# First-chunk hand-over in a one-core attention and ternary feed-forward kernel: later loads, stacks and one shift moved in the issue plan

## The chip, the core and the metric

The kernel runs on one core of one Trainium2 chip. Its time is the device time of one launch in microseconds (us), taken over several runs. One further run was profiled, and every row of a trace below is from that one execution. Engines: PE (TensorE), DVE (VectorE), ACT (ScalarE), POOL (GpSimd) and SP (the queue that issues most transfers).

## The reference

A block over 2048 tokens of 256 channels, cut to what matters:

```
xn  = layernorm(x)
q, k, v = xn@Wq, xn@Wk, xn@Wv         # 8 query heads, 2 key/value heads of 32
q, k = rope(q), rope(k)
out = softmax(causal(q k^T / sqrt(32))) @ v
geo = softmax(causal(qp[:,None] * kp[None,:])) @ v     # qp, kp: 3 channels of q, k on fixed directions
att = (out + scale_h * (geo - out)) @ Wo
z   = xn @ ternary(W_syn).T + b_syn   # 1024 wide
h   = relu(z) where z >= the 102nd largest of its row, else 0
ffn = layernorm(xn + h @ ternary(W_out).T + b_out) * gamma + beta
y   = x + att + ffn
```

## The kernel before, in words

The tokens are four chunks of 512 (`c`), each of four tiles of 128 (`t`). For each chunk the kernel normalizes x (`stat`, `eps`, `rstd`, `shift`, then `xn`), transposes it (`xT`, `xnT`), projects it (`qA`, `qB`, `qK`, `v`), rotates it (`rope`, `join`), splits q and k in a high and a low part (`khi`, `hi`, `klo`, `lo`), parks these in HBM and reads them back three times over as **stacks** (`stack_hi`, `stack_lo` into q_stack and k_stack), so that one matmul over 96 rows gives scores of full precision. A matmul `gx` gives the geometric rows, which are split (`geo_in`, `geo_hi`, `geo_lo`), scanned for running extremes (`scan`, `geo_top`) and copied by small transfers into k_geo and q_geo (`geo_rows`, `geo_dma`). A pass of 32 to 128 matmuls and DVE reductions per chunk (`S`, `red`) finds each row's maximum (`mT`, `m`). Then attention runs in 160 slots (chunk, head group, kind, key tile): `score` on PE, `exp` on ACT, a causal `cut` on POOL for diagonal tiles, and `val` and `sum` on PE. Kind 1, the geometric one, comes first in each chunk. The feed-forward part goes tile by tile beside it: `z` (PE, ACT), three `sign` passes on ACT that guess a threshold, `pick` and `hide` on DVE, `hT`, `h_hi`, `h_lo`, `fo`, then `y` on DVE and `y_out` on POOL, whose last line adds into res. The last chunk's output projection is the end.

The order of all this on every engine is a list made ahead by `build_plan`: a list scheduler that takes from each flow the key with the earliest start by written-in durations (a transfer also has a landing time in `LANDING`), and by rank where starts are close. Every engine then works its list strictly in order; what a key waits for at run time is the semaphores in the loops, not the plan's times. SP has one such list. Ahead of it stand some loads that are written out by hand: x of chunk 0, the small table, x of chunk 1, W_syn, and, in the kernel before, x of chunks 2 and 3, Wo, four broadcast rows (head scales, b_out, gamma, beta) and b_syn (together `late`). DVE's `w_sort` reorders Wq, Wk, Wv; `b_split` splits b_syn and is the first reader of the late loads; `w_next` loads W_out.

Lines of the profile that are named below: L1064 `stat`; L1080 to L1086 `w_sort`; L883 `xn`; L892 `xnT`; L968 `w_put`; L874 `t_put`; L576 `geo_rows` of the keys, which ACT issues in chunk 0 and SP later; L674 the same of the queries; L686 `geo_dma`; L653 and L656 the stacks; L1348 the projections; L1371 the `S` matmuls; L1175 and L1172 their reductions; L1234 the second half of `b_split`; L1426 the end of `fo`; L1311 `y`; L837 the end of `y_out`; L779 `cut`.

Of the kernel before, what the change touches and what calls it, by code (L numbers as in the profile page):

```python
# [12 lines left out]
P = 128  # L13
# [5 lines left out]
NCH = T // CHUNK  # L19
NT = T // P  # L20
TPC = CHUNK // P
# [24 lines left out]
           "xnT_park": 3500, "khi_park": 2200, "klo_park": 2200, "hi_park": 3500, "lo_park": 3500, "stack_hi": 8500,  # L46
           "stack_lo": 8000, "xz_in": 2300, "xb_in": 2300}
STAT_RANK = 3
# [16 lines left out]
def build_plan():  # L65
# [7 lines left out]
    def unit(flow, rank, name, ns, after=()):  # L73
        add(flow, "pe", rank, ("unit",) + name, ns, after, "full")
# [17 lines left out]
    for c in range(NCH):  # L92
# [5 lines left out]
        if c < 2:  # L98
            add("blank", "pool", 1, ("blank", c), 3600, [("rstd", c)])
        add("stat", "dve", STAT_RANK if c else 0, ("shift", c), 180, [("rstd", c)])  # L100
        for t in tiles:
            add("norm", "act", 1, ("xn", t), 400, [("shift", c)] + [("unit", "xT", c - 1, 1), ("xn_park", c - 1)] * (c > 0))
        add("park", "sp", 2, ("xn_park", c), 550, [("xn", t) for t in tiles])
# [6 lines left out]
        for s in "ABK":  # L110
            unit("proj", 2 * c, ("q" + s, c), 1790, [("xnT", c, 0), ("xnT", c, 1)] + [("w_sort",)] * (c == 0))
            add("rope", "dve", 0 if c == 0 else ROPE_RANK, ("rope", c, s), 1250, [("unit", "q" + s, c)] + [("t_put", c, i) for i in range(3)] + parked,
                empties=("q" + s, c))
        unit("proj", 2 * c, ("v", c), 1250, [("xnT", c, 0), ("xnT", c, 1)])
        add("v", "dve", 0.5, ("v_in", c), 350, [("unit", "v", c)], empties=("v", c))
# [37 lines left out]
        add("geo_k", "act" if c == 0 else "sp", 1, ("geo_rows", c, 0), 3300, [("geo_lo", c), ("geo_hi", c)])  # L153
        add("geo", "sp", 1, ("geo_rows", c, 1), 3300, [("geo_lo", c), ("geo_hi", c)] + used)
        add("geo", "sp", 1, ("geo_dma", c), 2200, [("geo_top", c)] + used)

# [20 lines left out]
    for t in range(NT):  # L177
        c = t // TPC
# [58 lines left out]

    done = {("x", 0): 5200.0, ("x", 1): 13000.0, ("x", 2): 19000.0, ("x", 3): 21000.0, ("ang_in", 0): 9500.0, ("dir_in",): 14000.0}
    done.update({("w",): 11000, ("late",): 26000, ("w_in", 0): 18000, ("w_in", 1): 19000})
    emptied_by = {}  # L240
# [97 lines left out]
def attention_and_ternary_ffn(nc, x, Wq, Wk, Wv, Wo, head_scales, W_syn, b_syn, W_out, b_out, gamma, beta,  # L338
# [25 lines left out]
    with ctx:  # L364
# [225 lines left out]
        def _(sp):  # L590
# [6 lines left out]
                         W_syn.rearrange("(a p) n -> p a n", p=P)).then_inc(up_in, 16)  # L597
            for c in range(2, NCH):
                sp.dma_start(res[:, TPC * c:TPC * c + TPC], x_rows[c]).then_inc(x_in[c], 16)
            sp.dma_start(w_o[:], Wo.rearrange("(g p) n -> p g n", p=P)).then_inc(late_in, 16)  # L600
            for t_, v_ in ((all_scales, head_scales), (b_down, b_out), (gam, gamma), (bet, beta)):
                sp.dma_start(t_[:], v_.rearrange("(o n) -> o n", o=1).broadcast_to([P, v_.shape[0]])).then_inc(late_in, 16)
            sp.dma_start(b_up, b_syn.rearrange("(o n) -> o n", o=1)).then_inc(late_in, 16)
            for key in plan["sp"]:
                k = key[0]
                if k == "m_dma":

                    c = key[1]
                    consumed(sp, ("mT", c))
                    for r, rows in enumerate((m_hi, m_lo)):  # L610
                        sp.dma_start(q_stack[STK + r:STK + r + 1, c % 2].bitcast(F32),
                                     rows.bitcast(F32)).then_inc(m_in[c], 16)
# [909 lines left out]
```

## Time and profile before

| what | value |
|---|---|
| median of 3 runs (lowest to highest) | 738.36 us (736.84 to 742.61) |
| the profiled execution's own time | 732.19 us |
| its span, first to last instruction | 730.3 us |
| around the span | 1.89 us |
| mean granted clock of TensorE | 0.974 of full speed |
| PE busy | 672.8 us |

The span is what the rows below add up to; the profiled execution was the fastest one shown, 6.2 us under the median. A busy PE is not one at its peak, since its matmuls overlap. The granted clock is a share: 0.50 is 1.2 GHz, 1.00 is 2.4 GHz.

### The profile page before, as it was taken

Reading aid. Unit: us, or ns where it says so; the run is one execution under the profiler, and the core shown is the slowest. Engines: PE = TensorE matmul, PEld = TensorE weight load, DVE = VectorE, ACT = ScalarE, POOL = GpSimd, SP = SyncE. Lnnn points to the kernel's source line nnn. Section 1 sums busy time; section 2 is a strip of 40 time slices with the busy share of each in tenths; the row PEclk is TensorE's granted clock in tenths of the full one; section 3 lists DMA queues with packets and bytes.
Section 4 is the critical chain, followed back from the end, with each engine's and each line's share of the span. In section 5 each row is a group of like instructions: output and inputs, shape, how many; then the busy total and the mean of one; then the engine's idle time right before and its main releaser. Section 6 shows DMA issues by size and latency. Waiting matters only on the chain. (4 is left out here: it accounts for less than half of the span.)

```text
span 730.3 us, 12339 instructions
## 1 busy us (share of the span) xinstructions
PE 672.8 (92%) x4424; PEld 317.3 (43%) x4424; DVE 497.2 (68%) x976; ACT 448.9 (61%) x732; POOL 238.3 (33%) x312
## 2 busy tenths in 40 slices
PE   4689898999899999998999999999899899997997
PEld 2443443434444443443434444454444455554443
DVE  7857996585768766778776776865675586766612
ACT  5435446455765444298744534789888879985553
POOL 5523445113213120232100121333443342346723
PEclk9979998999999999999999999999999899999999
DMA  8577000002700000053000000000001000000000
GB/s 241 191 190 195 11 9 1 30 2 92 189 9 2 1 1 1 3 153 63 1 5 1 1 1 1 19 29 22 23 23 31 22 22 23 16 23 9 1 1 30
DMA packets 26194, 30.81 MB, mean 42 GB/s; under 512 B 7105, under 2 KB 21313, under 8 KB 25746
## 3 DMA queue, kind: packets, MB, share of 16 engines
q1 hardware_dynamic: 24210, 29.45, 14.3%
q8 instruction: 36, 0.59, 0.3%
q10 hardware_dynamic: 1920, 0.54, 0.3%
q14 instruction: 28, 0.23, 0.1%
HBM read 17.72 MB, written 11.53 MB: 40 GB/s over the span
## 5 line engine op out<-in xcount | busy, mean ns | idle before, releaser
L935 ACT ACTIVATE probs<-scores 128x1024 f32<-128x1024 f32 (+3 forms) x320 | 270.9, 893 | 226.1 <-PE acc L1481 184.9
L1172 DVE TENSOR_REDUCE piece_max<-side 128x1 f32<-128x512 f32 x190 | 126.1, 685 | 61.3 <-PE side L1371 59.1
L1474 PE MATMUL acc<-probs,v_nat 128*32 128x512 f32 (+3 forms) x1280 | 151.9, 547 | 6.8 <-POOL probs L779 5.6
L1481 PE MATMUL acc<-probs,ones_all 128*32 128x512 f32 (+3 forms) x1280 | 152.0, 547 | 0.0
L1371 PE MATMUL side<-k_stack,q_stack 128*128 128x512 f32 (+3 forms) x316 | 120.9, 432 | 10.7 <-DVE piece_max L1172 3.2
L779 POOL TENSOR_SCALAR_AFFINE_SELECT probs<-probs 128x256 f32<-128x256 f32 x128 | 54.6, 436 | 226.3 <-ACT probs L935 225.0
L1371 PEld LDWEIGHTS side<-k_stack,q_stack 128*128 128x128 f32 x316 | 54.3, 188 | 101.3 <-DVE piece_max L1172 40.2
L1456 PE MATMUL scores<-q_stack,k_stack 128*128 128x512 f32 (+3 forms) x320 | 90.9, 387 | 5.3 <-ACT probs L935 4.9
L1175 DVE CUSTOM_DVE_ANT_0 side<-side,tail_mask 128x256 f32<-128x256 f32 (+3 forms) x126 | 61.8, 498 | 19.9 <-PE side L1371 19.2
L1474 PEld LDWEIGHTS acc<-probs,v_nat 128*32 128x32 f32 x1280 | 35.8, 111 | 78.8 <-issue 59.8
L1456 PEld LDWEIGHTS scores<-q_stack,k_stack 128*128 128x128 f32 x320 | 52.9, 190 | 36.9 <-ACT probs L935 29.8
L1460 PE MATMUL scores<-q_geo,k_geo 32*128 32x512 f32 (+3 forms) x320 | 54.2, 466 | 4.2 <-ACT probs L935 2.5
L1198 DVE RECIPROCAL d_raw<-d_raw 128x512 f32<-128x512 f32 x15 | 50.2, 3346 | 1.5 <-ACT d_raw L942 1.5
L1481 PEld LDWEIGHTS acc<-probs,ones_all 128*32 128x32 f32 x1280 | 29.5, 110 | 46.8 <-issue 44.3
L831 POOL TENSOR_TENSOR y_rstd<-y_mv,minus_half 128x1 f32<-128x1 f32 x16 | 10.4, 648 | 103.8 <-DVE y_mv L1315 103.6
L1460 PEld LDWEIGHTS scores<-q_geo,k_geo 32*128 32x128 f32 x320 | 22.3, 183 | 40.7 <-ACT probs L935 23.6
L1297 DVE SCALAR_TENSOR_TENSOR work<-z_buf,thresh 128x1024 f32<-128x1024 f32 x16 | 21.6, 1351 | 18.1 <-DVEq L1294 18.1
L1425 PE MATMUL side<-down_T,h_split 128*128 128x256 f32 x128 | 31.5, 285 | 1.9 <-DVE h_split L1304 1.9
L1304 DVE TENSOR_TENSOR h_split<-side,h_split 128x512 fp32r<-128x512 f32 x32 | 20.9, 678 | 15.9 <-ACT h_split L1029 15.9
L1426 PE MATMUL side<-down_T,h_split 128*128 128x256 f32 x128 | 30.9, 280 | 0.0
L1408 PE MATMUL side<-up_T,xs_hi 128*128 128x512 f32 x64 | 28.6, 447 | 1.2 <-DVE xs_lo L1241 0.5
L1425 PEld LDWEIGHTS side<-down_T,h_split 128*128 128x128 f32 x128 | 24.1, 188 | 7.5 <-issue 3.3
(170 smaller groups left out, 899.5 us busy)
## 6 DMA issues: line engine op xcount, KB each, us to landing
q_stack<-q_parked SPq DMA_DIRECT2D x12, 512.0 KB, 7.1
q_parked<-turned SPq DMA_DIRECT2D x8, 512.0 KB, 3.3
res<-in_L_attn_x_dram SPq DMA_DIRECT2D x4, 512.0 KB, 6.4
x_parked<-xn SPq DMA_DIRECT2D x4, 512.0 KB, 2.9
xT_parked<-xnT SPq DMA_DIRECT2D x4, 512.0 KB, 2.8
xz<-xT_parked SPq DMA_DIRECT2D x16, 128.0 KB, 2.5
xb<-x_parked SPq DMA_DIRECT2D x16, 128.0 KB, 2.2
out_dram<-res SPq DMA_DIRECT2D x16, 128.0 KB, 1.7
```

Of the source, the lines that this page charges most:

```text
L779: nc.gpsimd.affine_select(out=tri, in_=tri, compare_op=ALU.is_ge, fill=0.0, base=0, pattern=[[0, 2], [1, P]], channel_multiplier=-1).then_ ...
L935: nc.scalar.activation(probs[:, slot % 2, pair, :, off:], scores[:, pair, :, off:], ACT.Exp, scale=ATT_SCALE if kind == 0 else 1.0).then_i ...
L1172: free(nc.vector.tensor_reduce(piece_max[:, h, p:p + 1], pt, AX.X, ALU.max), ("S",) + a)
L1175: free(nc.vector.tensor_tensor_reduce(pt[:, 0:ncol], pt[:, 0:ncol], tail_mask[:, CHUNK - ncol:], 1.0, -3.0e38, ALU.add, ALU.max, piece_max ...
L1198: nc.vector.reciprocal(d_raw[:], d_raw[:]).then_inc(recip_ready, 1)
L1371: last = nc.tensor.matmul(pt[:, 0:ncol], q_stack[:, b, h, col:col + P], k_stack[:, h // HG, CHUNK * p:CHUNK * p + ncol], start=True, stop= ...
L1425: nc.tensor.matmul(pt[:, 0:C], h_hi[:, i], down_T[:, i], start=(i == 0), stop=False)
L1426: last = nc.tensor.matmul(pt[:, 0:C], h_lo[:, i], down_T[:, i], start=False, stop=(i == NN - 1))
L1456: last = nc.tensor.matmul(dst[:, off:], k_stack[:, g, P * j:P * j + P], q_stack[:, b, HG * g + h, off:], start=True, stop=True)
L1460: last = nc.tensor.matmul(dst[:, off:], k_geo[rows, P * j:P * j + P], q_geo[rows, g, off:], start=True, stop=True)
L1474: nc.tensor.matmul(acc[D * h:D * h + D, 0, off:], v_nat[:, j, g], probs[:, slot_no[a] % 2, h // 2, h % 2, off:], start=(j == 0), stop=(j = ...
L1481: last = nc.tensor.matmul(acc[D * h:D * h + D, 1, off:], ones[:, 0:D], probs[:, slot_no[a] % 2, h // 2, h % 2, off:], start=(j == 0), stop ...
```

## The change

The table and the rules of `build_plan` change, and with them the list of every engine. The loads of x for chunks 2 and 3 and the six late loads leave the hand-written start of SP's list and become keys that stand in SP's stack flow behind the first chunk's `stack_lo`, `geo_rows` and `geo_dma`. These two geometric steps of chunk 0 stand in the stack flow too. The second chunk's `shift` waits for the first chunk's rotation of k, its `xn` for `hi` of chunk 0, and its projections have rank 0.5 in place of 2. The times at which the plan takes x of chunk 1 and W_syn as landed are set earlier.

```diff
-           "stack_lo": 8000, "xz_in": 2300, "xb_in": 2300}
+           "stack_lo": 8000, "x": 5000, "late": 4000, "xz_in": 2300, "xb_in": 2300}
...
-        add("stat", "dve", STAT_RANK if c else 0, ("shift", c), 180, [("rstd", c)])
+        add("stat", "dve", STAT_RANK if c else 0, ("shift", c), 180, [("rstd", c)] + [("rope", 0, "K")] * (c == 1))
         for t in tiles:
-            add("norm", "act", 1, ("xn", t), 400, [("shift", c)] + [("unit", "xT", c - 1, 1), ("xn_park", c - 1)] * (c > 0))
+            add("norm", "act", 1, ("xn", t), 400, [("shift", c)] + [("hi", 0)] * (c == 1) + [("unit", "xT", c - 1, 1), ("xn_park", c - 1)] * (c > 0))
...
-            unit("proj", 2 * c, ("q" + s, c), 1790, [("xnT", c, 0), ("xnT", c, 1)] + [("w_sort",)] * (c == 0))
+            unit("proj", 0.5 if c == 1 else 2 * c, ("q" + s, c), 1790, [("xnT", c, 0), ("xnT", c, 1)] + [("w_sort",)] * (c == 0))
...
-        unit("proj", 2 * c, ("v", c), 1250, [("xnT", c, 0), ("xnT", c, 1)])
+        unit("proj", 0.5 if c == 1 else 2 * c, ("v", c), 1250, [("xnT", c, 0), ("xnT", c, 1)])
...
-        add("geo", "sp", 1, ("geo_rows", c, 1), 3300, [("geo_lo", c), ("geo_hi", c)] + used)
-        add("geo", "sp", 1, ("geo_dma", c), 2200, [("geo_top", c)] + used)
+        add("geo" if c else "stack", "sp", 1, ("geo_rows", c, 1), 3300, [("geo_lo", c), ("geo_hi", c)] + used)
+        add("geo" if c else "stack", "sp", 1, ("geo_dma", c), 2200, [("geo_top", c)] + used)
+        if c == 0:
+            for n in (2, 3):
+                add("stack", "sp", 1, ("x", n), 500)
+            add("stack", "sp", 1, ("late",), 4000)
...
-    done = {("x", 0): 5200.0, ("x", 1): 13000.0, ("x", 2): 19000.0, ("x", 3): 21000.0, ("ang_in", 0): 9500.0, ("dir_in",): 14000.0}
-    done.update({("w",): 11000, ("late",): 26000, ("w_in", 0): 18000, ("w_in", 1): 19000})
+    done = {("x", 0): 5200.0, ("x", 1): 10000.0, ("ang_in", 0): 9500.0, ("dir_in",): 14000.0}
+    done.update({("w",): 11000, ("w_in", 0): 16000})
...
-            for c in range(2, NCH):
-                sp.dma_start(res[:, TPC * c:TPC * c + TPC], x_rows[c]).then_inc(x_in[c], 16)
-            sp.dma_start(w_o[:], Wo.rearrange("(g p) n -> p g n", p=P)).then_inc(late_in, 16)
-            for t_, v_ in ((all_scales, head_scales), (b_down, b_out), (gam, gamma), (bet, beta)):
-                sp.dma_start(t_[:], v_.rearrange("(o n) -> o n", o=1).broadcast_to([P, v_.shape[0]])).then_inc(late_in, 16)
-            sp.dma_start(b_up, b_syn.rearrange("(o n) -> o n", o=1)).then_inc(late_in, 16)
             for key in plan["sp"]:
                 k = key[0]
+                if k == "x":
+                    c = key[1]
+                    sp.dma_start(res[:, TPC * c:TPC * c + TPC], x_rows[c]).then_inc(x_in[c], 16)
+                if k == "late":
+                    sp.dma_start(w_o[:], Wo.rearrange("(g p) n -> p g n", p=P)).then_inc(late_in, 16)
...
```

On SP, from the first chunk's parking to its geometric rows. Before (turned holds the split q and k, geo_rows and maxima the geometric rows):

```order
L632 DMA k_parked<-turned 64x512
L636 DMA q_parked<-turned 128x2x512
L632 DMA k_parked<-turned 64x512
L636 DMA q_parked<-turned 128x2x512
L674 DMA q_geo<-geo_rows 4x512 x6
L653 DMA k_stack<-k_parked 32x2x512 x2
L656 DMA q_stack<-q_parked 32x4096 x2
L653 DMA k_stack<-k_parked 32x2x512
L656 DMA q_stack<-q_parked 32x4096
L686 DMA q_geo<-maxima 4x512 x4
```

After, on SP at the same place:

```order
L642 DMA q_parked<-turned 128x2x512
L659 DMA k_stack<-k_parked 32x2x512 x2
L662 DMA q_stack<-q_parked 32x4096 x2
L629 DMA x_parked<-xn 128x4x256
L659 DMA k_stack<-k_parked 32x2x512
L662 DMA q_stack<-q_parked 32x4096
L680 DMA q_geo<-geo_rows 4x512 x6
L692 DMA q_geo<-maxima 4x512 x4
L606 DMA res<-in_L0_attn_x_dram 128x4x256 x2
L608 DMA w_o<-in_L0_attn_Wo_dram 128x2x256
```

The stacks went ahead of the six copies of L674, and x of chunks 2 and 3 and the late loads stand behind the geometric copies.

On ACT, from the first chunk's xnT (L892) to the first exponentials (L935). Before:

```order
L883 ACTIVATE xn<-res,shift,rstd 128x256 x4
L892 COPY xnT<-side 128x2x256 x2
L896 CAST turned<-turned 64x512
L901 CAST turned<-turned 128x1024
L910 COPY geo_rows<-side 8x512
L911 COPY geo_rows<-side 8x512
L922 CAST geo_rows<-geo_rows 8x1024
L968 CAST up_T<-side 128x512 x3
L576 DMA k_geo<-geo_rows 4x512 x6
L968 CAST up_T<-side 128x512
L874 COPY trig<-side 128x512 x3
```

After, on ACT at the same place:

```order
L902 CAST turned<-turned 64x512
L907 CAST turned<-turned 128x1024
L889 ACTIVATE xn<-res,shift,rstd 128x256
L916 COPY geo_rows<-side 8x512
L917 COPY geo_rows<-side 8x512
L928 CAST geo_rows<-geo_rows 8x1024
L889 ACTIVATE xn<-res,shift,rstd 128x256 x3
L974 CAST up_T<-side 128x512 x2
L580 DMA k_geo<-geo_rows 4x512 x6
L974 CAST up_T<-side 128x512 x2
L880 COPY trig<-side 128x512 x2
L898 COPY xnT<-side 128x2x256
```

The second chunk's four xn went behind `khi` and `hi`, and its two xnT behind the six issues of L576 (the second of them stands two rows further down); two w_put in place of one follow these issues.

On PE, the last 14 rows of scores, values and sums and the last tile of the feed-forward part. Before, the last `fo` (L1425, L1426) ends ahead of these rows:

```order
L1426 MATMUL side<-down_T,h_split 128x256
L1456 MATMUL scores<-q_stack,k_stack 128x512 x4
L1481 MATMUL acc<-probs,ones_all 32x512 x4
L1474 MATMUL acc<-probs,v_nat 32x512 x4
L1481 MATMUL acc<-probs,ones_all 32x512 x4
L1456 MATMUL scores<-q_stack,k_stack 128x512 x4
```

After, it ends ahead of these:

```order
L1432 MATMUL side<-down_T,h_split 128x256
L1462 MATMUL scores<-q_stack,k_stack 128x512 x4
L1487 MATMUL acc<-probs,ones_all 32x512 x4
L1480 MATMUL acc<-probs,v_nat 32x512 x4
L1487 MATMUL acc<-probs,ones_all 32x512 x4
L1462 MATMUL scores<-q_stack,k_stack 128x384 x4
L1462 MATMUL scores<-q_stack,k_stack 128x256 x4
L1480 MATMUL acc<-probs,v_nat 32x512 x4
```

Before, ten attention slots are left behind the last `fo`; after, six.

## Rows read from the trace of the kernel before

**Rows 1.** The page: span, PE's line of part 1, granted clock in 40 slices.
```profile
span 730.3 us, 12339 instructions
...
PE 672.8 (92%) x4424; PEld 317.3 (43%) x4424; DVE 497.2 (68%) x976; ACT 448.9 (61%) x732; POOL 238.3 (33%) x312
...
PEclk9979998999999999999999999999999899999999
```

**Rows 2.** Timeline from 0 us, all engines: start, us, engine, line, tiles [idle before].
```profile
6.88 0.38 SPq L595 DMA_DIRECT2D res<-in_L_attn_x_dram  x1
...
10.37 3.92 DVE L1080 COPY w_qkv<-probs 128x256 f32<-128x256 f32 x2
...
13.08 0.34 SPq L603 DMA_DIRECT2D z_buf<-in_L_ffn_b_syn_dram  x1
...
14.76 0.42 DVE L1064 BATCH_NORM_STATS2 stats<-res 128x6 f32<-128x256 f32 x1
...
15.43 0.43 DVE L1064 BATCH_NORM_STATS2 stats<-res 128x6 f32<-128x256 f32 x1
...
15.64 7.28 PE L1348 MATMUL side<-xnT,w_qkv 128*128 128x512 f32 x12 [0.77 <-ACT xnT L892]
...
20.57 2.07 ACT L883 ACTIVATE xn<-res,shift,rstd 128x256 f32<-128x256 f32 x4 [2.85 <-DMA x_parked<-xn]
...
25.86 1.07 ACT L892 COPY xnT<-side 128x512 f32<-128x512 f32 x2 [3.22 <-PE side L1340]
...
31.29 0.36 SPq L636 DMA_DIRECT2D q_parked<-turned  x1
...
32.54 3.78 SPq L674 DMA_DIRECT2D q_geo<-geo_rows  x6
32.54 4.92 ACTq L576 DMA_DIRECT2D k_geo<-geo_rows  x6
...
36.36 1.59 SPq L653 DMA_DIRECT2D k_stack<-k_parked  x2
...
39.78 1.21 DVE L1234 TENSOR_TENSOR b_up_r<-z_buf,b_up_r 1x1024 fp32r<-1x1024 f32 x1
...
40.76 2.25 SPq L686 DMA_DIRECT2D q_geo<-maxima  x4
```

**Rows 3.** Landing of L595, the load of x for chunk 1.
```profile
DMA to landing us min/median/max: 3.8/3.8/3.8
```

**Rows 4.** Timeline of PE from 36 us.
```profile
39.94 7.04 PE L1348 MATMUL side<-xnT,w_qkv 128*128 128x512 f32 x12
...
49.75 0.57 PE L1460 MATMUL scores<-q_geo,k_geo 32*128 32x512 f32 x4 [1.04 <-DMA q_geo<-maxima]
...
53.67 0.33 PE L1371 MATMUL side<-k_stack,q_stack 128*128 128x128 f32 x1
```

**Rows 5.** Window: us, busy PE, PEld, DVE, ACT, POOL (count), granted clock, DMA share, GB/s.
```profile
50.00:53.50 3.50, 3.50 (x8) 0.59 (x4) 0.00 (x0) 3.15 (x4) 0.87 (x3) 0.51 0.55 205
```

**Rows 6.** Timeline of PE from 312 us: `gx` of chunk 3 to its first `S`.
```profile
314.04 1.02 PE L1361 MATMUL side<-turned,dirs_k 128*40 128x512 f32 x2
...
334.90 0.70 PE L1371 MATMUL side<-k_stack,q_stack 128*128 128x512 f32 x2 [2.36 <-DMA q_stack<-q_parked]
```

**Rows 7.** Timeline of SP from 305 us.
```profile
325.07 0.57 SPq L656 DMA_DIRECT2D q_stack<-q_parked  x1
325.70 3.33 SPq L576 DMA_DIRECT2D k_geo<-geo_rows  x6
```

**Rows 8.** Window of the late stage, columns as in Rows 5.
```profile
500.00:700.00 200.00, 187.63 (x1361) 96.22 (x1357) 130.16 (x246) 160.22 (x293) 86.03 (x103) 0.97 0.06 19
```

**Rows 9.** Timeline of the last 40 us: y of the last tile, its end on POOL, the first cut behind it.
```profile
698.22 0.48 DVE L1311 SCALAR_TENSOR_TENSOR y<-side,w_scale,xb 128x256 f32<-128x256 f32 x1 [2.97 <-PE side L1426]
...
703.26 0.73 POOL L837 TENSOR_TENSOR res<-res,y 128x256 f32<-128x256 f32 x1
...
713.60 0.41 POOL L779 TENSOR_SCALAR_AFFINE_SELECT probs<-probs 128x256 f32<-128x256 f32 x1 [9.61 <-ACT probs L935]
```

More of the change, by code:

```diff
@@ L597, in _ @@
                          W_syn.rearrange("(a p) n -> p a n", p=P)).then_inc(up_in, 16)
-            for c in range(2, NCH):
-                sp.dma_start(res[:, TPC * c:TPC * c + TPC], x_rows[c]).then_inc(x_in[c], 16)
-            sp.dma_start(w_o[:], Wo.rearrange("(g p) n -> p g n", p=P)).then_inc(late_in, 16)
-            for t_, v_ in ((all_scales, head_scales), (b_down, b_out), (gam, gamma), (bet, beta)):
-                sp.dma_start(t_[:], v_.rearrange("(o n) -> o n", o=1).broadcast_to([P, v_.shape[0]])).then_inc(late_in, 16)
-            sp.dma_start(b_up, b_syn.rearrange("(o n) -> o n", o=1)).then_inc(late_in, 16)
             for key in plan["sp"]:
                 k = key[0]
+                if k == "x":
[3 more added lines that the diff above has]
+                    sp.dma_start(w_o[:], Wo.rearrange("(g p) n -> p g n", p=P)).then_inc(late_in, 16)
+                    for t_, v_ in ((all_scales, head_scales), (b_down, b_out), (gam, gamma), (bet, beta)):
+                        sp.dma_start(t_[:], v_.rearrange("(o n) -> o n", o=1).broadcast_to([P, v_.shape[0]])).then_inc(late_in, 16)
+                    sp.dma_start(b_up, b_syn.rearrange("(o n) -> o n", o=1)).then_inc(late_in, 16)
                 if k == "m_dma":
```

## The prediction

> **What bounds the kernel now.** I read the page first. PE is busy 672.8 of 730.3 us, and its matmuls fill every slice but the first few and the last, so the end is set by PE's list: time is gained where PE stands still or runs at half clock, nowhere else [rows 1]. Then the timeline of the first 60 us, engine by engine, since the diff acts there. What one should see is a ladder. DVE sorts the weights from 10.37 to 14.76 and the projections start at 15.64 [rows 2]. The second chunk's projections start at 39.94 and end at 48.7; PE then waits 1.04 us for the geometric rows, which SP had issued by 43.01 and which landed 6.7 us later [rows 2, 4]. Behind that gap the granted clock is 0.51 for 3.5 us, so that `gx` of chunk 1 runs at 1.2 GHz [rows 5]. The first `S` matmul comes at 53.67 [rows 4]. The third view is the border to chunk 3, where PE waits 2.36 us for stacks [rows 6], the fourth the late stage and the tail [rows 8, 9].
>
> **The loads that are moved.** From 7.26 to 13.42 SP issues nine loads in 6.2 us, W_syn's among them; eight of them, about 5.5 us, leave this place [rows 2]. Nobody waits for SP there: the first parking needs xn, and ACT's one wait on a transfer, 2.85 us for the parking of xn ahead of the second chunk's xn [rows 2], is no longer reached, since these xn now stand behind `hi` of chunk 0. Removing them is worth 0 by itself. In their new place they are issued from about 43.2 to 48.7 (the 5.5 us again), where SP had only the next angles and W_out to do.
>
> **The sort is later.** By the new list DVE takes two `stat` of chunk 1 ahead of `w_sort`. x of chunk 1 lands at 6.88 + 3.8 = 10.7 [rows 2, 3], two stats take 2 x 0.67 = 1.3 us (the step from 14.76 to 15.43), and the sort takes 4.4 us (10.37 to 14.76), so it ends at 16.4 in place of 14.76. PE, which started at 15.64, waits until 16.5: **+0.85 us**, on the path. It goes through rotations, joins and `gx` to `geo_lo`, which moves from 32.5 to 33.3. The second `shift`, which went behind the rotations, frees the first rotation from a wait for POOL, but with PE's projection late by the sort it has nothing to read sooner, so I count 0.
>
> **The stacks are earlier.** In the kernel before they are issued from 36.36, behind the six copies of L674 that take 3.78 us. Now they can go when the last parking is issued, 31.29 + 0.36 + 0.8 = 32.5, which is 3.9 us earlier [rows 2]. `geo_dma` stays behind all of it and ends near 43.2 as before (the issues are the same, only their order differs). So the stacks are there some 4 us sooner and the geometric rows at 48 to 50. This gains only what PE waited for: at most the 1.04 us of [rows 4], and only if PE is ready at 48.7.
>
> **ACT decides that it is not.** In the kernel before ACT has made both xnT of chunk 1 by 27, before the first chunk's splits. Now they come behind the six issues of L576, two `w_put` and three `t_put`. L576 cannot start before `geo_lo` at 33.3; I take 33.9, because one xn (2.07 / 4 = 0.52) went ahead of `geo_in`, and three xn and two `w_put` (1.55 + 1.07) fill the time behind `geo_hi`. The six issues hold ACT 4.92 us: 38.8. Seven copies of 1.07 / 2 = 0.535 follow, 3.75 us: 42.6 [rows 2]. The projections of chunk 1 start at 42.6 and not at 39.94: **+2.7 us**, with the +0.85 inside it. Bounds: if ACT issues at the rate at which SP did the same six at L576, 3.33 us [rows 7], and starts at 33.3, it is 40.4, or +0.5; were xn or a transpose late as well, a copy or two more, +3.7. I take the upper price of the issue, since it is the row of the same engine at the same place. The wait of 1.04 us then falls away, as the rows have landed by the time PE is done (8.8 us of projections, 51.4). The first score is 1.7 us later.
>
> The Trainium skill says, on the page "DMA: Bandwidth & Descriptors", section "Issuing engines are not separate DMA queues", that several issuing engines save only the sequencer's time for starting a transfer, usually small beside the transfer. The row speaks against "small" for copies of 8 KB: 4.92 us for six; were it nothing, the sum below would be 2.3 - 4.9 = -2.6 us.
>
> **The clock.** If PE comes from `v` straight to score and `S`, the half clock behind the gap should not occur: it cost half of 3.5 us, so **-1.7 us** [rows 5]. Nothing excludes that it falls there anyway: 0 to -1.7. I take -1.7, as the only thing before the fall is the gap.
>
> **The pass for the maxima.** Work done, not position, must be compared: at about 54 the new list has three `S` matmuls more behind it, and the balance of the terms so far, +2.7 - 1.0 - 1.7, is 0. Reductions start earlier, but `b_split` (its second half alone takes 1.21 us [rows 2]) stands now among them, on DVE, where before it ran at 39, ahead of the second chunk's rotations. PE has val and sum work mixed more evenly with `S`. I take 0, from -2 to +2.
>
> **The border to chunk 3.** The list puts `xT` and the projections of chunk 3 a slot later, and SP issues the six key rows (3.33 us) ahead of `stack_lo`, which it had issued by 325.64, ahead of them [rows 7]. PE's work from `gx` to the first `S` is nearly unchanged (one score and one sum more, two transposes less), so the 2.36 us wait stays [rows 6], and up to 2.7 us come on top (3.33 less one small read that leaves that place). The transfers of the first part are still under way then, which hides some of it: **+1.0 us**, from 0 to +2.7.
>
> **The tail.** The last `fo` stands six slots from the end and not ten. From there y and y_out take 703.99 - 698.2 = 5.8 us, and the cuts of the last four key tiles stand behind them on POOL. Before, POOL was idle for 9.61 us ahead of the first cut, at 713.60 [rows 9]. Now PE has a score, sum, val, sum and two short scores, about 5.4 us, before the value matmul that needs two cuts (2 x 0.41) behind 5.8 us. That is 6.7 against 5.4: **+1.3 us**, from 0 to +2.5.
>
> **The sum.** 2.7 - 1.0 - 1.7 + 0 + 1.0 + 1.3 = +2.3 us. On the profiled execution, 732.19 (span 730.3 and 1.89 around it), that is 734.5. The median of the runs is 6.2 us above that execution; against 738.36 it is **740.7 us**. A measurement of this kernel can tell about 1%, 7.4 us, from no change, so this is a forecast of no change.
>
> **Rivals.** First, **faster**, near 730. The issues on ACT cost 3.3 us (-1.6 or more), the even mix of `S` saves 2 us, no term at the border or in the tail (-2.3), and one or two of the other stretches of half clock, 1.7 us each, do not occur. For it: the page shows a clock under 0.9 in slices 3, 7 and 32 [rows 1], and none of these is tied to work that must stay. Against it: the head has only 1.04 us of waiting that the change names, and its gain is eaten by ACT.
>
> Second, **slower**, near 750: the feed-forward part is crowded. The new list runs the `z` of tile 3 after slot 102 where it was slot 64, and the later tiles 4 to 10 slots later, but ends only 4 later. In the late stage ACT is busy 160.2 and PE 187.6 of 200 us; PE stands 12.4 us [rows 8]. One more tile there is 8 us or so of ACT's signs, copies and relu by my estimate from what is left of ACT (40 us). It decides when the chain sign, pick, hide, hT, fo of a tile is longer than the attention work that the list put between; then PE's 12.4 us double, +12. Against it: the mean leaves room, and the list interleaves by durations near the real ones.
>
> Third, **the loads come late**, 744. `b_split` waits for b_syn, the last of the loads, issued at about 48.7. By L595, 3.8 us [rows 3], it lands at 52.5, before DVE gets there at about 53.5, and costs nothing; by the 6.7 us of the geometric rows in a full queue, and x, Wo and W_out are 2.6 MB around it, at 55.4 or later. All reductions behind it in DVE's list wait, then PE for its two banks: 2 to 4 us, over the forecast. The Trainium skill, same page, section "Rules for kernel authors", advises to issue a transfer early and wait late; it speaks against this part of the change. By that rule the result would be this rival's.
>
> Fourth, the change doesn't do what it says: the stacks' landing gates nothing, because the projections fill PE until 51. That is inside the forecast.
>
> **How the numbers follow.** Forecast 0.47, within 735 to 746; faster 0.20; slower 0.18; loads late 0.15. Low end: 740.7 less 1.6, 2, 2.3 and three stretches of clock (5) gives 729.8, and the 1% bound is 731.0; high end: 740.7 + 1.7 + 2 + 1.7 + 1.2 + half of the crowding, 6, gives 753. From 730 to 752 leaves out some 2 in 10. Faster by over 1% (under 731.0) 0.15, within 1% 0.63, slower (over 745.7) 0.22.
>
> **What would show it.** Right: the projections' first pass near 16.5 and, for chunk 1, between 42 and 43, behind ACT's L580; stacks issued at 32.5; no wait for q_geo ahead of the first score; clock 1.00 near 52; a wait on POOL's cut in the last 15 us. Wrong: chunk 1's projections at 40.5 or sooner; a DVE idle row ahead of `b_split`, released by a transfer; PE busy under 92% between 500 and 700 us.

## The result, and the profile after

The changed kernel takes 728.86 us (median of 4 runs, 725.67 to 730.76) where the kernel before takes 737.6 us (4 runs, 735.14 to 742.61): a ratio of 0.9873, interval 0.9831 to 0.9915. I had forecast 740.7 us and a range whose lower end was 730. The profiled executions lie much closer together, 730.06 against 732.19 us, so first the rows, then what separates medians and profiles.

The page of the changed kernel, answering to [rows 1]:

```profile
span 728.3 us, 12341 instructions
...
PE 676.6 (93%) x4424; PEld 318.3 (44%) x4424; DVE 495.3 (68%) x976; ACT 448.2 (62%) x732; POOL 230.8 (32%) x312
...
PEclk9788887999999999999999999999999999999999
```

PE is busy 3.8 us longer in a span that is 2.0 us shorter: it stands 51.7 us in place of 57.5, and more of its time is at half clock. The first slices are no better than before, so the gain must be elsewhere.

The timeline of the first 55 us, answering to [rows 2] and [rows 4]; ACTq and SPq are the issues of transfers:

```profile
9.70 3.51 POOL L768 MEMSET q_stack<- 32x4096 f32 x1
...
11.60 2.06 DVE L1086 COPY w_qkv<-probs 128x256 f32<-128x256 f32 x2
...
15.36 5.40 PE L1354 MATMUL side<-xnT,w_qkv 128*128 128x512 f32 x6 [0.77 <-ACT xnT L898]
...
32.25 1.34 SPq L659 DMA_DIRECT2D k_stack<-k_parked  x2
33.10 1.25 ACTq L580 DMA_DIRECT2D k_geo<-geo_rows  x1
...
34.38 2.96 ACTq L580 DMA_DIRECT2D k_geo<-geo_rows  x5
...
43.03 5.39 PE L1354 MATMUL side<-xnT,w_qkv 128*128 128x512 f32 x12 [0.77 <-ACT xnT L898]
...
50.08 0.51 PE L1466 MATMUL scores<-q_geo,k_geo 32*128 32x512 f32 x4
...
53.20 0.69 DVE L1239 CAST b_up_r<-z_buf 1x1024 fp32r<-1x1024 f32 x1 [1.18 <-DMA z_buf<-in_L_ffn_b_syn_dram]
```

The first projection starts at 15.36, 0.28 us earlier than before, and waits for xnT, not for the sort. The stacks are issued at 32.25, as computed. The second chunk's projections start at 43.03 behind ACT's six issues (42.6 was forecast), the first score has no wait, and DVE stands 1.18 us for b_syn.

Windows of the changed kernel: the first score, the border to chunk 3, the late stage (answering to [rows 5] and [rows 8]):

```profile
50.00:53.50 3.50, 3.17 (x14) 1.15 (x13) 1.84 (x9) 2.88 (x4) 2.09 (x3) 1.00 0.86 215
...
300.00:345.00 45.00, 43.61 (x284) 19.36 (x282) 30.57 (x48) 29.52 (x48) 10.81 (x11) 1.00 0.38 97
...
500.00:700.00 200.00, 191.97 (x1382) 98.25 (x1378) 137.00 (x258) 174.34 (x329) 89.48 (x107) 0.98 0.07 22
...
660.00:700.00 40.00, 39.24 (x297) 19.28 (x297) 31.17 (x58) 31.13 (x48) 24.72 (x26) 1.00 0.04 11
```

The same windows of the kernel before:

```profile
300.00:345.00 45.00, 41.29 (x263) 19.72 (x253) 34.60 (x54) 32.90 (x57) 12.64 (x9) 1.00 0.37 88
660.00:700.00 40.00, 35.48 (x268) 18.32 (x272) 25.01 (x43) 19.94 (x26) 22.50 (x23) 0.96 0.01 4
```

PE stands 2.3 us less at the border, 3.8 us less between 660 and 700, and 2.0 us less between 600 and 660. That is 8.1 us where the whole span gives 5.8: between 500 and 600 it stands 1.4 us more (92.90 us busy, before 94.29), and elsewhere the windows hold different work. ACT is busier in the last of these windows, 31.1 of 40 us against 19.9: feed-forward work that the old order had already finished now stands beside the short diagonal slots. In the old order PE waits there for POOL, for ACT, and once for the feed-forward part's own split on DVE:

```profile
661.39 1.51 PE L1474 MATMUL acc<-probs,v_nat 128*32 128x384 f32 x8 [1.77 <-POOL probs L779]
...
670.95 0.73 PE L1456 MATMUL scores<-q_stack,k_stack 128*128 128x512 f32 x2 [1.20 <-ACT probs L935]
...
681.60 0.36 PE L1425 MATMUL side<-down_T,h_split 128*128 128x256 f32 x1 [1.21 <-DVE h_split L1304]
```

Whom PE waits for from 500 us to the end (us in total, times, longest), first before, then after:

```profile
PE acc L1474 <- POOL probs L779: 4.3, 4, 2.1
PE scores L1456 <- ACT probs L935: 2.0, 3, 1.2
PE scores L1460 <- ACT probs L935: 1.2, 1, 1.2
PE side L1425 <- DVE h_split L1304: 1.9, 2, 1.2
PE side L1385 <- DVE onehot L1265: 0.9, 2, 0.7
```

```profile
PE acc L1480 <- POOL probs L785: 2.6, 4, 1.6
PE scores L1466 <- ACT probs L941: 2.0, 5, 0.6
PE scores L1462 <- ACT probs L941: 1.0, 3, 0.4
PE side L1422 <- DVE work L1303: 1.4, 3, 0.6
PE side L1414 <- DVE xs_lo L1247: 1.1, 2, 0.7
```

The waits for `probs`, those that other work beside them could fill, fall from 7.5 to 5.6 us. Over the whole span they do not fall: the same view without a window adds up to 13.0 us before and 13.5 after. What the end gained in this way, other places lost. What fell over the whole span are the waits for `h_split` (3.9 to 0.9 us), for the angles that POOL copies into `turned` (5.2 to 0.8, 3.0 of it in the first 40 us), for the stacks (2.4 to 0.2) and for q_geo (1.0 to 0).

At the border, the timeline of PE after, answering to [rows 6], with SP's list behind it, answering to [rows 7]:

```profile
323.36 1.05 PE L1366 MATMUL side<-turned,dirs_q 128*40 128x512 f32 x2
...
332.12 3.34 SPq L580 DMA_DIRECT2D k_geo<-geo_rows  x6
...
336.20 0.58 SPq L662 DMA_DIRECT2D q_stack<-q_parked  x1
...
342.90 0.70 PE L1377 MATMUL side<-k_stack,q_stack 128*128 128x512 f32 x2 [0.21 <-DMA q_stack<-q_parked]
```

The key rows do go ahead of `stack_lo`, but PE's wait is 0.21 us and not 2.36. From the last stack's issue to the end of the wait it is 6.7 us (342.90 less 336.20), where it was 9.8 (334.90 less 325.07). PE's work between `gx` and this matmul did not grow: it is busy 18.2 us there (324.25 to 342.90) and was busy 18.0 (314.04 to 334.90).

In the tail, the last y_out, the cuts behind it, and PE, answering to [rows 9]:

```profile
712.08 0.73 POOL L843 TENSOR_TENSOR res<-res,y 128x256 f32<-128x256 f32 x1
712.76 1.49 POOL L785 TENSOR_SCALAR_AFFINE_SELECT probs<-probs 128x256 f32<-128x256 f32 x4
...
713.58 1.06 PE L1480 MATMUL acc<-probs,v_nat 128*32 128x512 f32 x8 [0.28 <-POOL probs L785]
```

**Medians and profiles.** Each run's record has the mean granted clock. Over 86 runs of before, slow ones left out, its mean is 0.962, over the ten of the changed kernel 0.967. These 86 runs show what the clock is worth: a line through them falls by 4.6 us for each 0.01 of it. So the clock is 2.3 us of the 9, and at equal clock the changed kernel is 7.1 us under that line. PE standing less is 4 to 6 us of it (55.5 to 57.5 us against 51.3 to 51.7, two profiles of each). The first profile of before, at 0.974, was a lucky one: by the same line that is 5.5 of the 6.2 us to the median.

### The profile page after: what moved, and what is told of

Its sections match the earlier page's. It is cut to its first block, busy times and chain, and to the rows that moved or that the text cites. A ratio compares the mean times of both kernels' runs of the same rounds, so it can differ in the third digit from the quotient of the medians.

```text
span 728.3 us, 12341 instructions
## 1 busy us (share of the span) xinstructions
PE 676.6 (93%) x4424; PEld 318.3 (44%) x4424; DVE 495.3 (68%) x976; ACT 448.2 (62%) x732; POOL 230.8 (32%) x312
## 4 chain that ended last, share of the span: by engine, by line
PE 71%; DVE 9%; ACT 6%; POOL 5%; issue 4%; DMA 3%; SPq 1%; ACTq 1%; DVEq 0%; POOLq 0%
PE acc L1487 15%; PE acc L1480 15%; PE side L1377 11%; PE scores L1462 7%; PE scores L1466 4%; DVE piece_max L1178 4%; ACT probs L941 3%; PE side L1354 3%; PE side L1441 2%; PE side L1431 2%; PE side L1414 2%; PE side L1422 2%; PE side L1432 2%; PE side L1415 1%; DVE side L1181 1%
## 5 line engine op out<-in xcount | busy, mean ns | idle before, releaser
L1466 PEld LDWEIGHTS scores<-q_geo,k_geo 32*128 32x128 f32 x320 | 22.0, 184 | 42.6 <-ACT probs L941 29.1
L807 POOL TENSOR_TENSOR mixed<-o_raw,d_raw 128x512 f32<-128x512 f32 x8 | 10.2, 1279 | 61.3 <-DVE d_raw L1204 61.2
```

The costliest lines, as they stand in the source:

```text
L1466: last = nc.tensor.matmul(dst[:, off:], k_geo[rows, P * j:P * j + P], q_geo[rows, g, off:], start=True, stop=True)
```

## The experiments

All ratios are to the kernel before, with 95% intervals; kernels were run on the same chip as their runs of before. The profile's time of one execution is named only where it matters. The planner was given a switch for each part of the change: loads, stacks, shift, xn, proj, and times (the landing times of x of chunk 1 and W_syn set earlier). A *splice* takes the first keys of one order and the rest of another. FIRST and REST name the parts switched on in the two orders, ALL stands for all six, and UNTIL is the key at which they change over (the edits are shown in short form):

```diff
+    head = order[:order.index(UNTIL)]        # of the first order
+    fixed = head + [key for key in then if key not in head]   # then: the second order
+    plan = plan_by(FIRST, fixed)             # keys in this order on every engine
```

**The two kernels again**, unchanged.

> The changed kernel once more, on the same chip and beside the same runs of before as the two halves. All theories: 0.983 to 0.992. Its profile shows how much of the clock's half-speed stretches (47.8 us in the first profile) and of PE's idle time (51.7 us) repeats from one execution to the next: idle within 1 us, half-speed stretches anywhere from 35 to 60 us.

> The kernel before once more. Ratio 0.997 to 1.003. Theory A: PE's busy time is 5 us above the first profile's 672.8 us, by more half-speed stretches, since that execution was 5 us faster than the median; the idle time is within 1 us of 57.5 us. Rival B: it has more idle time, in the first 100 us, than the first profile showed.

0.9866 (0.9818 to 0.9914) and 1.0003 (0.9966 to 1.0039). The profile of before had PE busy 677.9 us (5.1 more than the first), standing 55.5; that of the changed kernel 678.8 and 51.3. The gain repeats. The standing repeats within 2.0 us for before, where 1 us had been expected, and within 0.4 us for the changed kernel. The extra busy time of before goes with a lower clock, 0.965 against 0.974, as theory A had it.

**Which half?** Head new up to slot 61 and late order old, then the reverse.

```diff
+FIRST, REST, UNTIL = ALL, (), ("score", 2, 1, 1, 2, 0)      # head_new
+FIRST, REST, UNTIL = (), ALL, ("score", 2, 1, 1, 2, 0)      # late_new
```

> The plan of the change up to slot 61 (c 2, head group 1, geometric, key tile 2, at about 300 us), and from there the order of the kernel before. Theory A, formed from the two traces: the gain lies behind this slot, since PE's idle time fell by 2.3 us between 300 and 345 us and by 5.7 us between 600 and 700, and only by 0.9 us in the first 60; then this kernel takes what the kernel before takes, ratio 0.997 to 1.004. Rival B: the gain lies in the first chunk's hand-over, and the profiled execution of before happened to be a good one there; then the ratio is that of the whole change, 0.985 to 0.991. Rival C: the new head costs what I predicted for it (sort +0.85, ACT +1.85, wait -1.0, clock -1.7): 1.000.

> The other half: the order of the kernel before up to slot 61, loads by hand at the start of SP's list included, and from there the order of the change. Theory A (the gain is in the new order of the late part): ratio 0.985 to 0.992. Rival B (it is in the head): 0.997 to 1.004. If both halves give some 4 us each, 0.994 and 0.994, the gain is a sum of two.

0.9981 (0.9948 to 1.0015) and 0.9990 (0.9961 to 1.0019): neither half had the gain. In head_new PE does not wait for a stack at the border at all, so the 2.36 us of that wait do not make the gain by themselves. The windows show that the second splice made a hole of its own at the border, though its late window is dense:

```profile
300.00:345.00 45.00, 39.41 (x241) 16.75 (x241) 28.55 (x46) 20.78 (x31) 7.97 (x9) 0.92 0.23 60
660.00:700.00 40.00, 39.43 (x300) 21.37 (x289) 29.86 (x57) 35.41 (x66) 24.60 (x28) 1.00 0.05 14
```

**The splice put where the two orders nearly coincide** (slot 27).

```diff
+FIRST, REST, UNTIL = (), ALL, ("sum", 1, 1, 1, 2)
```

> The order of before for the first two chunks (up to slot 27, some 180 us, the early loads included), the order of the change from there. The first attempt at this half changed over at slot 61, in the middle of the third chunk's hand-over, and its trace shows a hole of its own there: PE 39.4 of 45 us busy between 300 and 345 (43.6 in the changed kernel), gx of chunk 3 waiting 2.16 us behind a feed-forward unit, and two half-speed stretches behind it; yet 98.3 of 100 us busy between 600 and 700 (99.1 in the changed kernel, 93.3 before). Theory A, the gain is in the order behind the first two chunks: 0.986 to 0.993. Rival B, it needs the new head: 0.996 to 1.003. Rival D, the two need each other: also near 1.00, but then its window from 600 to 700 is below 96 us busy.

0.9870 (0.9827 to 0.9913): the whole gain, with the old head, its late sort, its late stacks and its early loads. Its windows are those of the changed kernel:

```profile
300.00:345.00 45.00, 43.09 (x285) 18.91 (x283) 29.75 (x47) 30.58 (x48) 10.44 (x10) 1.00 0.38 97
...
660.00:700.00 40.00, 39.08 (x295) 19.21 (x297) 31.15 (x58) 31.34 (x48) 24.72 (x27) 1.00 0.04 11
```

**Parts of the change, without a splice.** Two parts alone, and all but one.

```diff
+FIRST = ("loads", "stacks")                              # stacks_loads
+FIRST = ("times", "loads", "stacks", "shift", "proj")    # no_xn
```

> Two of the five parts: the loads and x as keys behind the stacks, and the geometric rows behind the stacks; shift, xn, the projections' rank and the two times stay as before. The planner gives with these two parts the late order of the changed kernel (from the third chunk on the same). Theory A: the whole gain, 0.983 to 0.991, whatever the head does. Rival B (the head's xn and projections carry it): 0.996 to 1.003.

> All parts of the change but one: the second chunk's xn does not wait for hi of chunk 0. The planner then falls back into the order of before from the second chunk's attention on, with the stacks ahead, the late loads, the shift and the rank of the change in its head. Theory A: no gain, 0.996 to 1.004. Rival B: 0.985 to 0.991.

stacks_loads: 0.9878 (0.9851 to 0.9906), as expected of the new late order. But no_xn is slower than before by 1.4% (1.0137, 1.0103 to 1.0171), which neither theory had. Its late order is the old one, and its first two chunks cost the 10 us: `gx` of chunk 2 starts at 197.2, where the two profiles of before have 180.9 and 184.0, and the distance stays the same from there. With `shift` behind the rotation and nothing to hold xn, ACT runs the four xn, both xnT and the split of the geometric rows ahead of `hi`, which moves from about 27 to 32.99; q_parked, the stacks and the next angles follow, and PE waits. Some 4 us are lost by 55 us; the rest comes behind it, where PE waits among others 5.0 us for POOL's probs.

```profile
38.76 1.12 PE L1429 MATMUL side<-ident,h_split 128*128 128x128 f32 x4 [4.62 <-ACT up_T L999]
41.71 1.94 PE L1364 MATMUL side<-ident,turned 128*128 128x128 f32 x8 [1.83 <-POOL turned L611]
```

So the xn part, which I had charged with the delay of the second chunk, is what keeps the other parts from costing 10 us, as far as this one kernel shows.

**The feed-forward tiles alone.** Before, with a table of slots behind which each tile may start; then only the last four tiles.

```diff
+    at = (17, 62, 63, 100, 99, 103, 102, 113, 118, 114, 114, 117, 123, 124, 126, 129)   # z_late
+        turn.append(slots[at[t] - 1])
+    for t, at in ((12, 130), (13, 136), (14, 137), (15, 140)):                          # tail_late
+        turn[t] = slots[at - 1]
```

> The kernel before, all loads and the first chunk's order as they were, with one table added: the slot behind which each feed-forward tile may start, chosen so that z and fo of every tile stand in the slots where the changed kernel has them (first fo at slot 65 for 63, the rest the same, the last at 154). From chunk 3 on its PE order is that of the changed kernel. Theory A in its sharper form: the gain is that feed-forward work is left as filler for PE in the half-empty diagonal slots near 660 us and behind them: between 600 and 700 us PE is busy 98 to 99 us, ratio 0.988 to 0.995. Rival B: 0.997 to 1.004.

> The kernel before with four numbers added: tiles 12 to 15 of the feed-forward part may start only behind slots 130, 136, 137 and 140. The PE order is that of before up to slot 124; the z of these tiles then stands at slots 132, 137, 140 and 142 (before 128, 131, 134, 137) and the last fo at slot 153 (before 150, changed kernel 154). If filler work behind 655 us is what the change gained: PE is busy 37 to 39.5 us of 40 between 660 and 700 (before 34.6 to 35.5), and the ratio is 0.991 to 0.996. If the gain lies at the border and in the middle, the ratio is 0.997 to 1.003, though the window may fill.

0.9964 (0.9940 to 0.9987) and 0.9971 (0.9944 to 0.9998): each about a quarter of the gain, below what theory A asked for, and the second only just clear of no change. From the maxima pass of chunk 3 on PE's list in z_late is that of the changed kernel, so most of the gain is not in that order alone. In tail_late the window from 660 to 700 fills to 38.54 of 40 us as expected, but the one from 600 to 660 falls to 56.88 (before 57.86 and 58.71), where the tiles held back are missing.

```profile
600.00:660.00 60.00, 56.88 (x399) 30.02 (x399) 36.99 (x69) 46.88 (x81) 22.61 (x29) 0.97 0.08 23
660.00:700.00 40.00, 38.54 (x282) 20.39 (x280) 29.93 (x53) 34.04 (x62) 21.45 (x22) 1.00 0.03 8
```

**More splices in chunk 3**, meant to tell the border from the stretch behind 600 us: the new order only from slot 96, only up to slot 96, and only up to slot 128.

```diff
+FIRST, REST, UNTIL = (), ALL, ("score", 3, 0, 1, 0, 0)      # late_new3
+FIRST, REST, UNTIL = ALL, (), ("score", 3, 0, 1, 0, 0)      # mid_new
+FIRST, REST, UNTIL = ALL, (), ("score", 3, 0, 0, 0, 0)      # tail_old
```

> The order of before for three chunks (up to slot 96, the first geometric slot of chunk 3), then the order of the change. It keeps the old border to chunk 3 with its wait of 2.36 us and two feed-forward tiles done early, and has the new places of tiles 4 to 15. Theory A as it stands: PE is busy 98 to 99 us between 600 and 700, which is 5 us less standing, and the ratio is 0.989 to 0.994. If the kernel with its z slots pinned (0.9964, also dense there) tells what this stretch alone is worth, it is 0.995 to 0.998 and the rest of the gain lies in the middle, from the third chunk's pass to the border.

> The order of the change up to slot 96, the new border to chunk 3 included, then the order of before, whose feed-forward tiles end at slot 150. If the dense stretch behind 600 us carries the gain: 0.994 to 1.000, with PE at 93 to 94 us busy between 600 and 700. If the border and the middle carry it: 0.986 to 0.991.

> The order of the change up to slot 128 (about 594 us), then the order of before: the tile that is behind is caught up at once, and the last ten slots have no feed-forward work beside them. If the stretch behind 600 us carries the gain: PE is busy 93 to 95 us between 600 and 700 and the ratio is 0.993 to 0.999. If the gain was made before slot 128: 0.986 to 0.990.

1.0014 (0.9975 to 1.0052), 1.0100 (1.0050 to 1.0150), 1.0104 (1.0070 to 1.0137): all three lost something at the junction, and don't decide. late_new3 has PE busy 64.32 of 70 us between 450 and 520; tail_old falls to 25.57 of 30 us between 600 and 630; mid_new has a long stretch at half clock where its splice is, with a PE that the row calls busy nearly throughout:

```profile
455.00:480.00 25.00, 24.35 (x77) 9.55 (x78) 19.19 (x31) 9.38 (x18) 0.60 (x1) 0.52 0.02 6
660.00:700.00 40.00, 34.87 (x265) 18.80 (x264) 27.76 (x47) 25.10 (x44) 22.83 (x28) 0.96 0.03 11
```

One thing holds in every kernel: those that end in the new order have PE busy 39.1 to 39.7 of 40 us between 660 and 700, those that end in the old one 34.5 to 36.1. But late_new and late_new3 are among the first, at 39.4, and have no gain: a full window at the end is not enough.

**SP's list in the changed kernel.** Loads at its start again; the six query rows ahead of the stacks again; both.

```diff
+    plan["sp"] = loads + [key for key in plan["sp"] if key not in loads]      # early_loads
+    sp.insert(sp.index(("stack_hi", 0)), ("geo_rows", 0, 1))                  # geo_first
```

> The changed kernel with every list as it is, but x of chunks 2 and 3 and the six late loads issued at the start of SP's list, as before. By my rival of the loads that come late, DVE's wait of 1.18 us for b_syn goes and with it at most 1.2 us: 0.984 to 0.987 where the changed kernel has 0.987. If the place of the loads costs and gives nothing: 0.985 to 0.990. If the gain of the change were that the first transfers are not crowded by these loads: 0.992 or more.

> The changed kernel with one key moved on SP: the six copies of the geometric query rows go ahead of the first chunk's stacks again, which are then issued from 36 and not from 32 us. By the prediction the stacks' landing gates nothing, since PE is busy with the projections until 50: ratio 0.985 to 0.990, first S within 1 us. If the earlier stacks carry something: 0.991 or more, and a wait for a stack ahead of the first S.

> Both edits of SP's list together, the loads at its start and the six query rows ahead of the stacks. If geo_first lost its 5 us because it pushed b_syn later (DVE waited 4.13 us for it), they are back: 0.983 to 0.988. If the stacks' place counts by itself: 0.990 or more.

0.9832 (0.9800 to 0.9864), 0.9927 (0.9899 to 0.9955), 0.9853 (0.9805 to 0.9901). geo_first lost half a per cent, and its trace has no wait of PE for a stack behind the first score, but one of DVE for b_syn. The load is not asked for later than in the changed kernel (at 48.47, there 48.70); DVE goes on 9.0 us behind its issue, there 4.5 us, with the transfer engines 1.01 busy in the mean between 40 and 57 us:

```profile
57.42 0.69 DVE L1242 CAST b_up_r<-z_buf 1x1024 fp32r<-1x1024 f32 x1 [4.13 <-DMA z_buf<-in_L_ffn_b_syn_dram]
```

With the loads early as well, `b_split` starts at 52.95 without a wait and the loss is gone:

```profile
52.95 0.68 DVE L1244 CAST b_up_r<-z_buf 1x1024 fp32r<-1x1024 f32 x1
```

The stacks' place by itself shows no worth; what cost was a late load asked for while the transfers were that dense. The changed kernel with its loads early has the lowest ratio of all, a little under the 0.984 that I had expected at best, but its interval overlaps that of the changed kernel: on these runs it is at least as good, and not shown better.

**POOL's clearing and the sort.**

```diff
+    pool.insert(pool.index(("rstd", 1)) + 1, ("blank", 0))
+    pool.insert(pool.index(("join", 0, "K")) + 1, ("blank", 1))
```

The second clearing also waits for the join ahead of it, and early_blank is this with the early loads.

> The changed kernel with POOL's two clearings of q_stack rows moved: the first (3.51 us) behind rstd of chunk 1, at about 16 instead of 9.70 us, the second behind the first chunk's joins. In both traces DVE's two copies of the sort end 0.45 us after this clearing ends. If the clearing holds them, they take some 0.9 us for two (a copy of the same shape takes 0.42 at L1134) in place of 2.06, and the sort ends at 12.5 to 13.0. If their time is their own, 2.06 stays. Either way the first projection waits for xnT (15.2), so the time stays: 0.985 to 0.990; if the sort had been what held the projections, 1 us less.

> The changed kernel with the loads at the start of SP's list and POOL's clearings later. The first edit takes a DVE wait of about 1 us away, the second has shown no gain alone: 0.982 to 0.986, at most 1 us under the changed kernel with early loads alone.

0.9851 (0.9811 to 0.9891) alone and 0.9847 (0.9796 to 0.9899) with the early loads: no gain in time, as expected. But the sort's two big copies take 0.67 us in place of 2.06 (before: 3.92):

```profile
11.66 0.67 DVE L1092 COPY w_qkv<-probs 128x256 f32<-128x256 f32 x2
```

## Why the prediction was wrong, step by step

- **The sort is later, +0.85.** Wrong, and not only in size: the first projection is 0.28 us earlier. I gave the sort the 4.4 us that it took before, and 3.9 of them were two copies that ran beside POOL's clearing. In the changed kernel the sort begins 1.2 us later and ends at 14.21; the first projection waits for ACT's xnT anyway.
- **The stacks are earlier, worth only PE's wait.** Right: issued at 32.25 (32.5 forecast), no wait for q_geo, and early_geo, where they are issued from 36.73, has 0.9853 against 0.9832 with the loads early alone, a difference inside the intervals.
- **ACT decides, +2.7.** The mechanism was right and the start of 43.03 is near the 42.6 forecast. But what followed was not 8.8 us of projections. The clock was 1.00 from 43 to 50 us, where before had 0.77 from 39.9 to 47, and the twelve projections took 5.39 us against 7.04: I had used a duration that held half clock. The first score is at 50.08, 0.33 later than before, and not 1.7.
- **The clock, -1.7.** Right at that place (1.00 between 50.0 and 53.5), but the head as a whole got worse: the clock of the first 190 us is 0.89 and 0.87 in the two profiles of the changed kernel, 0.95 and 0.91 in those of before, and behind 190 us it is 0.99 against 0.98. That I priced one stretch and forecast the rest as staying was the error.
- **The border to chunk 3, +1.0.** Wrong in sign: -2.2. The key rows go first, as I said, and PE's work up to the first `S` is unchanged, as I said (18.2 us against 18.0). But behind `gx` the last stack is issued only 0.9 us later (12.0 us behind it, before 11.0), and PE goes on 6.7 us behind that issue and not 9.8. I had kept the landing and added the issues. Why it lands sooner was not tested; before, the six key rows followed it at once.
- **The tail, +1.3.** The mechanism was right (the cuts start at 712.76, right behind y_out), the size was 0.28.
- **The rival that the feed-forward part is crowded.** This is the step that failed most. I read the late stage as a mean, ACT 160 of 200 us, and asked only whether more work would fit. It fits, and the standing between 500 and 700 went from 12.4 to 8.0 us, between 660 and 700 from 4.5 to 0.8. The trace of before had a sign of it: a window of 40 us in place of 200 shows ACT at 19.9 and PE waiting at the diagonal slots. My sum has no term for the move of these tiles, and as a rival I gave it a negative price alone. What the new order saves is only in part such filling, as the waits above show.
- **The rival "faster, near 730".** It had the time (728.86, outside the range by 1.1 us) and a chance of 0.20, with reasons that came true in part: ACT's issues took 4.2 us (1.25 and 2.96), not 3.3, and the tail cost little. The border did not stay at nothing but gained, and the late order was not among its reasons.
- **The loads come late.** The mechanism was right, its size small in this kernel: DVE stood 1.18 and 0.61 us in two profiles, and not at all in head_new and stacks_loads, which have the same late loads. It is near a larger loss, as geo_first shows with 4.13 us. The Trainium skill's advice to issue early and wait late, "DMA: Bandwidth & Descriptors", section "Rules for kernel authors", agrees with that run.
- **The base.** I added the sum to the median and wrote that the profiled execution was 6.2 us under it, without asking what made it so. Most of it was the clock, 0.974 against 0.962 in the mean of the runs. Two of the half-clock stretches of before, at 190 and 661 us, stand behind waits of 2.20 and 1.77 us, and the changed kernel has neither. But a wait does not always bring one: behind the 2.36 us at the border the clock stayed at 1.00. The first of these waits in the timeline of before (the second is shown above), and the windows of the two stretches and of the border:

```profile
189.50 0.63 PE L1333 MATMUL side<-ident,turned 128*128 128x128 f32 x4 [2.20 <-POOL turned L582]
```

```profile
190.00:193.40 3.40, 3.40 (x11) 2.56 (x9) 3.26 (x7) 0.25 (x1) 2.45 (x3) 0.50 1.11 265
661.10:664.50 3.40, 3.11 (x24) 1.11 (x28) 3.37 (x5) 0.20 (x1) 1.65 (x4) 0.51 0.00 0
334.00:338.00 4.00, 2.81 (x17) 1.20 (x17) 2.22 (x4) 3.76 (x9) 0.73 (x1) 1.00 0.05 11
```

In short: the forecast was +2.3 us and the change took some 9 us off. The terms that failed are the border (+1.0, where PE stood 2.15 us less) and the late order, which the sum had at nothing and the second rival at a loss, where PE stood 4.3 us less between 500 and 700.

**What is shown and what stays open.** Shown: the gain lies in the order behind slot 27 and needs no part of the new head (late_new2), and two of the parts bring this order about (stacks_loads). Also shown: the changed kernel and head_new are the same up to slot 61 and differ by 1.1% behind it. Holding back the last four tiles gives about a quarter of the gain. Open: by which waits the new order gains, and how the gain divides between chunk 2, the border, chunk 3 and the clock. Each splice there made a loss of its own, and z_late, whose PE stands as little as the changed kernel's in its profile (730.3 less 678.9, 51.4 us), has a ratio 0.9% higher, some 7 us; its clock in the mean (0.965 against 0.967) explains 1 us of it.

## What to carry to other kernels

Where an order is made by a greedy planner, an edit at the start is an edit everywhere: compare the two orders over the whole program, and read the windows of the far places before those of the near one. Work on a side chain can be filler for the engine that bounds, so ask of each later place not only whether the work fits there, but whether that engine now stands there for lack of it, in windows as short as the stretch, and then where the work will be missing. Add up the waits over the whole span as well: a window that fills can have been paid for by another. And a duration from a trace is a price only if nothing ran beside it that won't run beside it in the new place.

## What the hardware showed that I had not expected

While POOL's MEMSET of 32 x 4096 ran (3.51 us), DVE's copies of 128x256 were held: two took 3.92 us when they began with it (10.37, the clearing at 10.32), 2.06 us when they began 1.9 us into it, each time ending 0.45 us behind its end, and 0.67 us without it. DVE's statistics of the same tile size were not held: 0.43 us during the clearing and 0.43 without it. And half clock can last: 25 us at 0.52 in mid_new, where the changed kernel is at 1.00 throughout the windows from 345 to 520. The 24.35 us busy in that row overstate the work. Just ahead of it, from 448 to 455 us, PE was busy 3.9 of 7 us; from 455.5 to 467.2 its fifteen `S` matmuls start 0.78 us apart, each behind a reduction on DVE of 0.69 us, so the row counts as busy what is paced by DVE. From 467.2 to 480 PE worked densely, 62 matmuls in 12.8 us, and the clock was still 0.51. Why it stayed there was not found.
